# An LSTM with a generated adapter on one core: x loaded one block sooner, the adapter weight in row pieces

## The reference

```python
# x: (16, 256, 256) as batch, time, feature; cond: (16, 256)
xz = einsum('ntd,dk->ntk', x, Wx) + b                 # for all time steps
def step((h, c), xz_t):                               # 256 steps, one after the other
    ai, af, ao, ag = split(xz_t + h @ Wh, 4, axis=1)
    c = sigmoid(af) * c + sigmoid(ai) * tanh(ag)
    h = sigmoid(ao) * tanh(c)
x = x + hs                                            # hs: all h, h0 = cond
cn = layernorm(cond) * gamma + beta
hid = gelu(cn @ W1 + bias1)                           # (16, 256)
w = hid @ W2 + bias2                                  # W2: (256, 8192), 8 MB
a1, b1, a2, b2 = [t.reshape(16, 256, 8) for t in split(w, 4, axis=-1)]
mid = gelu(x @ base_down + (x @ a2) @ b2^T)           # rank-8 adapter for each sequence
x = x + mid @ base_up + (mid @ b1) @ a1^T
```

## Time and profile before

| | |
|---|---|
| median of 3 runs | 603.57 us (603.19 to 603.63) |
| the profiled execution | 603.59 us |
| its span, first to last instruction | 601.6 us |
| TensorE matmul busy | 582.8 us, 97% of the span |
| VectorE / ScalarE busy | 83% / 64% |
| SP's DMA queue (q1) | 39456 packets, 37.01 MB |
| W2 transfers | 32 of 256 KB |

### The profile page before, as it was taken

One profiled execution on the slowest core, in us unless ns is written; L12 is line 12 of the kernel. 1 busy time (PEld: TensorE's weight loads), 2 busy tenths in 40 slices (PEclk: granted clock), 3 DMA queues, 4 the chain that ended last, 5 costly groups with the idle time before them and its releaser, 6 DMA issues.

```text
span 601.6 us, 34256 instructions
## 1 busy us (share of the span) xinstructions
PE 582.8 (97%) x14110; PEld 438.2 (73%) x14110; DVE 502.3 (83%) x2809; ACT 384.6 (64%) x2154; POOL 47.4 (8%) x91
## 2 busy tenths in 40 slices
PE   8887989999999999999999999999999999999997
PEld 7654567777777777777777777777777777777885
DVE  4776978888888888888888888888888888888873
ACT  2554656666666666666666666666666666666663
POOL 3002130000000000000000000000000000000000
PEclk9999999999999999999999999999999999999999
DMA  6998893311332312223232123332212323211301
GB/s 193 173 189 171 175 170 52 50 33 33 56 56 55 57 40 41 35 57 56 56 56 38 33 44 57 56 56 56 37 32 48 54 57 56 57 33 21 55 20 29
DMA packets 40157, 39.74 MB, mean 66 GB/s; under 512 B 4369, under 2 KB 38977, under 8 KB 40002
## 3 DMA queue, kind: packets, MB, share of 16 engines
q1 hardware_dynamic: 39456, 37.01, 33.9%
q0 software_dynamic: 512, 0.53, 0.5%
q10 hardware_dynamic: 34, 0.02, 0.0%
HBM read 16.05 MB, written 4.19 MB: 34 GB/s over the span
## 4 chain that ended last, share of the span: by engine, by line
PE 92%; DMA 3%; DVE 2%; issue 1%; SPq 0%; ACT 0%; POOL 0%; POOLq 0%; ACTq 0%
PE z L701 35%; PE x_bank L491 17%; PE z_o L701 9%; PE aux L520 8%; PE out_bank L547 7%; PE aux L504 3%; PE aux L472 2%; PE out_bank L579 2%; PE aux L527 2%; DMA x_nat<-in_x 2%; PE out_bank L622 1%; PE out_bank L568 1%; DMA seed<-proj 1%; PE x_bank L568 1%; PE x_bank L520 0%
## 5 line engine op out<-in xcount | busy, mean ns | idle before, releaser
L701 PE MATMUL z<-wh,h_t 128*16 128x96 f32 x8160 | 234.6, 248 | 3.5 <-DVE h_t L880 1.9
L701 PEld LDWEIGHTS z<-wh,h_t 128*16 128x16 f32 x8160 | 153.1, 96 | 109.0 <-DVE h_t L880 80.4
L855 DVE STREAM_TRANSPOSE z<-z 128x96 f32<-128x96 f32 x512 | 152.5, 298 | 67.9 <-PE z L701 42.5
L417 ACT ACTIVATE gates<-z 128x48 f32<-128x48 f32 x512 | 108.1, 211 | 120.2 <-DVE z L855 119.9
L491 PE MATMUL x_bank<-wx,x_t 128*128 128x256 f32 x512 | 152.6, 385 | 0.6 <-ACT x_t L347 0.5
L353 ACT ACTIVATE z<-seed 128x96 f32<-128x96 f32 x512 | 127.0, 248 | 6.2 <-DMA seed<-proj 6.2
L701 PE MATMUL z_o<-wh,h_t 128*16 128x64 f32 x4080 | 105.0, 219 | 0.7 <-issue 0.7
L865 DVE SCALAR_TENSOR_TENSOR prod<-gates 128x32 f32<-128x32 f32 x512 | 98.5, 192 | 2.3 <-ACT gates L417 2.0
L491 PEld LDWEIGHTS x_bank<-wx,x_t 128*128 128x128 f32 x512 | 78.8, 192 | 4.1 <-ACT x_t L347 0.7
L701 PEld LDWEIGHTS z_o<-wh,h_t 128*16 128x16 f32 x4080 | 80.2, 97 | 1.2 <-issue 0.9
L357 ACT ACTIVATE z_o<-seed 128x64 f32<-128x64 f32 x256 | 58.3, 228 | 19.3
(11 more groups left out here) (127 smaller groups left out, 520.8 us busy)
## 6 DMA issues: line engine op xcount, KB each, us to landing
seed<-proj SPq DMA_DIRECT2D x128, 128.0 KB, 4.4
w<-in_L_cond_W SPq DMA_DIRECT2D x33, 256.0 KB, 5.2
x_nat<-in_x SPq DMA_DIRECT2D x32, 128.0 KB, 4.0
out<-y_nat SPq DMA_DIRECT2D x32, 128.0 KB, 4.1
wx<-in_L_cond_Wx SPq DMA_DIRECT2D x2, 256.0 KB, 3.7
wx<-in_L_cond_Wx SPq DMA_DIRECT2D x1, 512.0 KB, 4.3
wh<-in_L_cond_Wh SPq DMA_DIRECT2D x2, 256.0 KB, 5.3
wh<-in_L_cond_Wh SPq DMA_DIRECT2D x1, 512.0 KB, 6.2
```

Of the source, the lines that this page charges most:

```text
L417: act.activation(gates[s % 2][m][:, 0:3 * B].rearrange("p (g b) -> p g b", b=B), zt[m].rearrange("p (g c) -> p g c", c=C)[:, :, 0:B], ACT. ...
L701: ins = pe.matmul(dst, h_prev[:, kc, :], rhs, start=False, stop=(kc == 1), skip_group_check=True)
L855: dve.transpose(zt[m], z_bank[m][:, 0:GC]).then_inc(turned[m], 1)
```

## The change

The loads of x move one block forward: block 4's stands among block 0's W2 transfers (behind piece 4), and block k issues that of block k+4. A piece of W2 is no longer one column half of one contraction half but 32 partitions' rows of both contraction halves, over all 2048 columns of the quarter: two transfers of 256 KB again, one for each contraction half, now 32 rows of 8 KB. The first product of a quarter waits for all eight transfers of the quarter, its other three steps for none.

```diff
--- before.py
+++ after.py
@@ -145,7 +145,7 @@
         zeroed = sem("zeroed")
         w_loaded = {n: sem(f"{n}_loaded") for n in
                     ("wx_g", "wx_if", "wx_o", "wh_g", "wh_if", "wh_o", "b", "down", "up", "ln", "cond", "w1")}
-        w2_loaded = [[[sem(f"w2_loaded{q}_{i}_{r}") for r in range(2)] for i in range(NQ)] for q in range(4)]
+        w2_loaded = [[[sem(f"w2_loaded{q}_{i}_{kc}") for kc in range(2)] for i in range(NQ)] for q in range(4)]
         w_bias_zeroed, w_bias_loaded = sem("w_bias_zeroed"), sem("w_bias_loaded")
         w_placed = [sem(f"w_placed{q}") for q in range(4)]
         wx_ready, wh_ready = sem("wx_ready"), sem("wh_ready")
@@ -264,20 +264,19 @@
                 sp.dma_start(dst[:, :, lo:lo + n], src.rearrange(by_half, m=NM)[:, :, src_lo:src_lo + n])\
                   .then_inc(w_loaded[name], 16)
 
-            w2_parts = W2.rearrange("(k p) (q j h n) -> q h k p j n", p=P, q=4, j=NQ, n=W_HALF)
+            w2_rows = W2.rearrange("(k i p) (q n) -> q i k p n", k=2, i=NQ, q=4)
 
             def load_w2(piece):
 
                 n, i = divmod(piece, NQ)
-                q, (h, kc) = QUARTERS[n], divmod(i, 2)
+                q = QUARTERS[n]
                 if piece == 3 * NQ:
                     sp.wait_ge(w_psum, 2)
-                for r, rows in enumerate((slice(0, P // 2), slice(P // 2, P))):
-                    back, half = divmod(2 * piece + r - UNDER_WAY, 2)
+                for kc in range(2):
+                    back, kc_back = divmod(2 * piece + kc - UNDER_WAY, 2)
                     if back >= 0:
-                        sp.wait_ge(w2_loaded[QUARTERS[back // NQ]][back % NQ][half], 16)
-                    sp.dma_start(w2[q][rows, kc, :].rearrange("p (j h n) -> p h j n", j=NQ, n=W_HALF)[:, h],
-                                 w2_parts[q, h, kc, rows]).then_inc(w2_loaded[q][i][r], 16)
+                        sp.wait_ge(w2_loaded[QUARTERS[back // NQ]][back % NQ][kc_back], 16)
+                    sp.dma_start(w2[q][32 * i:32 * (i + 1), kc, :], w2_rows[q, i, kc]).then_inc(w2_loaded[q][i][kc], 16)
 
             bias_q = bias2.rearrange("(q j n) -> j q n", q=4, j=NQ)
 
@@ -308,10 +307,14 @@
                 if not k.at_least(1):
                     load_w2(0)
                     load_w2(1)
-                if k.plus(3).exists():
+                if not k.at_least(1):
                     load_x(k.plus(3))
+                elif k.plus(4).exists():
+                    load_x(k.plus(4))
                 for piece in {0: range(2, 8), 1: range(8, 13), 2: range(13, 4 * NQ)}.get(k.k, ()):
                     load_w2(piece)
+                    if piece == 4:
+                        load_x(k.plus(4))
                     if 2 <= piece < 2 + NQ:
                         load_w_bias(piece - 2)
                 if front:
@@ -615,8 +618,10 @@
                         pe.wait_ge(up_ready, 2)
                     elif kc == 0:
                         pe.wait_ge(w_biased, 2 * n + h)
-                    for half in w2_loaded[q][i]:
-                        pe.wait_ge(half, 16)
+                    if i == 0:
+                        for part in w2_loaded[q]:
+                            for half in part:
+                                pe.wait_ge(half, 16)
                     for j in range(NQ):
                         first = W_COLS * j + W_HALF * h
                         ins = pe.matmul(out_bank[32 * j:32 * j + B, 0:W_HALF], hid[:, kc, :],
```

## The result

The kernel after takes 611.22 us (median of four runs, 609.41 to 612.72) against 603.6 (603.19 to 603.77) for the kernel before beside it: a ratio of 1.0118, 95% interval [1.0095, 1.0141]. The change makes the kernel 1.2% slower.

A forecast was written before the change was run, and what follows sets the result against it. TensorE ends the chain for 92% of the span; only the first 90 us, where W2 comes in, could change. Step 23's wait swallows earlier terms: 603.59 + 7.3 = 610.9 us, range 604.5 to 618.5.

The forecast's parts named there:

- x one block sooner, keeping 0.3 us: Steps 15 and 23: x waits of 3.13 and 0.98 us go; late seeds in step 15 leave 0.3 us gain.
- Step 19 waits 3.1 us: Step 19's W2 product waits 3.1 us for transfer d23, landing at 70.8 us; step 20 begins 2.8 us later.
- Step 23 waits 5.5 us; step 24 begins 7.3 us later: Step 23's product waits for the last W2 transfer, d31, landing at 86.5 us; this wait swallows the earlier terms.
- Row transfers at an unchanged pace: W2 stream: 32 rows of 8 KB take 1.42 us per 256 KB, as before; d31 moves 19 us per 1 us.
- fast bound: W2 stream: 0.73 us per 256 KB, as transfers onto 128 partitions; -0.7 us each, d31 13 us sooner.
- Rival 2: W2 stream: rows come in faster, d31 at 73.5 us, no new wait, 599.5 to some 601 us; chance 0.11.
- Rival 3: W2 stream: rows come in slower, +0.3 to +0.9 us each, d31 6 to 17 us later, 617 to 628; chance 0.13.
- Nothing for the clock in the sum: Behind step 23's wait: the forecast sum adds no time for TensorE at half speed.
- Rival 1: Step 23: TensorE's clock falls in the 5.5 us wait, to half speed, 1.2 instead of 2.4 GHz; chance 0.19.
- The 2 us for the clock in the high end of the range: High end, 618.5 us: 2 us for the clock added beside 5.7 us for slower row transfers.
- From 90 us on as before: After W2 has come in: every step runs as before; gain or loss by 90 us stays to the end.

The follow-up runs named there:

- wait alone: Kernel before, its column pieces and loads of x kept, with only the wait for a whole quarter of W2 added: 611.64 us, ratio 1.0120.
- rows on 128 partitions: Kernel after with each W2 transfer as 2 KB of each of 128 rows, not 8 KB of 32; waits and sooner x kept: 604.56 us, ratio 1.0007.

## Why the prediction was right, point by point

The prediction was 610.9 us, slower, in a range of 604.5 to 618.5; it came out at 611.22. That the median lies so near is in part luck: the profiled execution, which the account below follows, took 612.72, and the forecast left out a loss that it shows.

- *x one block sooner, keeping 0.3 us.* Right. Both waits went, the seeds held step 15, and step 16 began 0.7 us sooner (58.69 against 59.37). By itself the part is worth nothing that can be measured. The prediction named the seeds; it did not see the "issue" waits, which took a share too.
- *Step 19 waits 3.1 us.* Mechanism right, size 2.23: d23 was issued at 65.17 us, not 65.57, and landed in 4.5 us, not 5.2. What no step said is that the clock fell behind it.
- *Step 23 waits 5.5 us; step 24 begins 7.3 us later.* Right: 5.65, and the product starts 6.92 us later, as d31 landed at 86.0 us and not 86.5. The wait alone, on the old column pieces, makes the same loss, so this is the cause.
- *Row transfers at an unchanged pace.* Right: 186 against 184 GB/s, d31 issued 0.5 us sooner. A faster stream exists, but it belongs to 128 partitions and not to 8 KB rows: 213 to 217 GB/s came with 1 KB and with 2 KB runs. That is some 1.2 us for 256 KB, far from the fast bound of 0.73. What the pace does to d31 was set too small: with 0.2 us less for each transfer d31 was issued 7 us sooner, some 35 us for each 1 us by this estimate, where the prediction had 19. Rival 2's turning point, d31 at 79.2 us, fits "rows on 128 partitions", where d31 landed at 79.4 and the time was that of before (1.0007). Rival 3 did not come.
- *Nothing for the clock in the sum.* This is the term that was mis-sized: it was put at nothing, and the profiled execution lost 2.25 us by it, with a mean clock of 0.988 to 0.994 in all four runs. Rival 1 had the fall, at a chance of 0.19. The 2 us for the clock in the high end of the range had no run behind them; the 2.25 us are what the runs show in their place, read from steps 23 to 26 at either level. What the prediction set against the fall was that a wait of 3.13 us had left the clock full in the kernel before; a wait of 2.23 us in step 19 then lowered it, and the 3.27 us for x in "wait alone" did too (0.74 granted from 50 to 60 us). One wait without a fall proved nothing: of 51 executions of the kernel before that were run beside the experiments, 13 had a mean granted clock of 0.991 to 0.994, with a median of 605.8 us against 603.4 for the other 38. The profiled execution is therefore 1.8 us over the forecast, 2.25 less the 0.4 by which d31 was early.
- *From 90 us on as before.* Right but for the tail of the clock's fall: from step 26 on there is no difference.

## What to carry to other kernels

Look at what a consumer needs first: transfers whose order of arrival matches the order of use hide a late end of the stream, and a reshaping that makes the first use wait for the last byte gives that up, here 1.2%, however long the runs. Here it was width that paid and not length: all 128 partitions for each transfer were worth 0.7 to 0.8% with the bytes and packets unchanged, and moved the late loads forward without touching the order. Removing a wait is worth only what the next late thing leaves of it.

## What had not been expected of the hardware

- Six transfers of 256 KB under way in place of three cost 12 us with rows (623.01 against 611.22) and 14 with columns (618.00 against 604.31): TensorE stopped for up to 5.13 us in the middle of its gate matmuls with no wait on another engine or on W2, each stop ending 2.7 to 3.0 us after a packet of the instruction queue.
- The clock fell behind a wait of 2.23 us (step 19, products at half speed one step later), and stayed full behind one of 3.13 us in the profiled execution of the kernel before; in 13 of 51 other executions of that kernel the mean granted clock was 0.994 or less.
- The last of 32 equal transfers took between 4.2 and 7.7 us to land in the kernels with 32 or 64 partitions and three under way. A wait for it carries that spread into the time.
